# Causal masks of the second chunk moved from matmuls to GpSimd selects, and half-width scores for the last diagonal blocks

## The chip, the cores and the metric

One core of a Trainium2 chip runs the whole program. The metric is the device time of one execution in microseconds. The core has TensorE (PE in the rows, PEld for its weight loads), VectorE (DVE), ScalarE (ACT), GpSimd (POOL) and SyncE (SP), which here only issues transfers. Each engine works through its own instruction list strictly in the order in which it was written.

## The reference

The program is a layer on x of shape 4 x 1024 x 256. First comes a recurrence over the 1024 time steps, then attention with 16 heads of width 16, then four expert networks weighed by a gate:

```python
state = jnp.tanh(p_t + state)                      # 1024 steps, one after the other
scores = jnp.einsum('bhqd,bhkd->bhqk', q, k) * HD ** (-0.5)
scores = jnp.where(causal[None, None], scores, -jnp.inf)
attn = jax.nn.softmax(scores, axis=-1)
ao = jnp.einsum('bhqk,bhkd->bhqd', attn, v)...
x = x + ao
o0 = gelu(xf @ e0_up.T) @ e0_down.T;  o1 = silu(xf @ e1_w1.T) * (xf @ e1_w2.T) @ e1_down.T
o2 = gelu(gelu(gelu(xf @ e2_l1.T) @ e2_l2.T) @ e2_l3.T) @ e2_l4.T
o3 = gelu(gelu(xf @ e3_down.T) @ e3_up.T) @ e3_out.T
moe = wts[:, 0:1] * o0 + wts[:, 1:2] * o1 + wts[:, 2:3] * o2 + wts[:, 3:4] * o3
```

A query attends to the keys up to its own position only. That causal mask is what the change is about.

## The kernel before

Time is cut into four chunks of 256 steps, and with four batches that makes 16 units u of 256 rows. Chunk c holds the units 4c to 4c+3. Chunk 0 is laid out differently: its units hold 128 rows of two batches each. A unit goes through these items, named as in the code: `pgate` (VectorE multiplies the states by their gate, L1414, once the chunk's states are there), `ptr` (TensorE transposes the result, tensor G), the projections, keys and queries (`qk`, `kt`, `qt`), the row maxima of the scores (`mxm` on TensorE, `mxr` on VectorE, L1502), the scores again in transposed form (`sc`), their exponentials (`ex`, ScalarE L996), their product with the values (`av`), the gate, and the expert networks (`up`, `dn`, `gel` with Gelu, ScalarE L1021). The recurrence runs beside all that: `sadd` on GpSimd (L1703, 128x8) and `stanh` on ScalarE (L928) take turns 1023 times.

An item ("sc", u, g, kb) computes, for the four heads of group g of unit u, the scores of 128 keys (key block kb) against the unit's 256 queries: four matmuls of 64 rows and 256 columns (QT,KT in the rows), two for each half of the array's rows. Two of the key blocks of a unit of chunks 1 to 3 lie on the diagonal: r = kb - 2c = 0, where the first 128 queries are masked, and r = 1, where the first 128 queries see none of the keys and only the other 128 are masked and used. `ex` and `av` of r = 1 already work on the 128 later queries alone. The key blocks of an item lie in one of three buffers PT, which `sc` takes and `av` frees.

The mask is made in two ways. In chunks 0 and 1 TensorE adds a large negative triangle to the scores, with bf16 matmuls of 128 rows and 256 columns (maskk,identb; two for each diagonal block in chunk 1). In chunks 2 and 3 GpSimd sets the exponentials above the diagonal to zero with a select (item `msk`, L1710), between `ex` and `av`.

The order of each engine's list is made at build time by a planner, `arrange`: each item has a cost and a due time, and the planner plays the engines against each other and picks, whenever one is free, the ready item that is due first. Due times are START[u] plus an offset of the table AT for the kind of item and the chunk; STAY is a penalty for a change of the tile shape on TensorE (64 rows for scores, 128x32 for `av`, 128x128 for the rest) or of the activation table on ScalarE (exp and tanh against Gelu). What comes out is a fixed list for each engine with semaphore waits.

Of the kernel before, what the change touches and what calls it, by code (L numbers as in the profile page):

```python
# [14 lines left out]
L = 256  # L15
# [39 lines left out]
WINDOW, LOW, HIGH, FRESH = 3.413, 0.38, 0.75, 80.0  # L55

STALL = {"wsh": 0.3, "wsp": 0.45, "gll": 0.45, "kh": 0.12, "pgate": 0.15, "qq": 0.06, "hsc": 0.05, "fin": 0.05, "pln": 0.03, "pu": 0.03}
STAY = {"pe": 16.7, "act": 8.9}

START = (102.9, 140.3, 204.6, 251.3, 335.0, 429.5, 526.1, 598.9, 741.5, 802.0, 921.2, 978.2, 1089.0, 1179.7, 1287.1, 1381.6)  # L60
AT = {"piece": (39.4, 44.9, 92.6, 23.9),
      "post": (93.2, 49.6, -17.0, 3.1),
      "prep": (-51.0, -38.4, -68.0, -35.2),
      "value": (-95.0, 23.8, -123.9, -82.3),
      "key": (-43.2, -59.1, -16.5, -80.5),
      "query": (-41.3, -15.2, -108.7, -61.0),
      "max": (-17.8, -44.1, -58.3, -51.2),
      "maxima": (-1.8, 0.3, 14.4, 28.3),
      "bound": (89.2, -27.2, 53.0, 56.2),
      "score": (35.5, 43.9, 31.6, 47.9),  # L70
      "scores": (10.8, 11.3, 14.8, 8.7),
      "av": (16.9, -18.8, -3.1, 1.4),
      "merge": (20.7, -9.4, 0.4, 0.6),
      "out": (-126.5, -10.3, -47.2, -91.6),
      "gate": (-4.1, -106.5, -67.1, 55.1),
      "l1": (80.1, 225.4, 181.2, 220.9),
      "e0up": (150.5, 178.4, 131.2, 276.8),
      "l2": (216.7, 249.6, 193.5, 235.9),
      "e0dn": (276.2, 242.4, 399.5, 7.6),
      "e1": (250.8, 267.7, 297.6, 287.7),  # L80
      "l3": (312.5, 277.6, 195.7, 216.8),
      "e3dn": (206.3, 290.6, 219.8, 294.3),
      "e1dn": (324.7, 305.2, 239.5, 272.0),
      "l4": (309.9, 294.0, 253.9, 336.6),
      "e3up": (322.5, 265.2, 244.9, 238.0),
      "e3out": (277.8, 251.8, 317.6, 371.2),
      "fin": (272.9, 230.9, 245.5, 366.3)}


class Plan:  # L90
# [6 lines left out]
    def add(self, engine, key, us, due, *after, take=None, mode=None, lat=0.0):  # L97
        self.items[key] = (engine, us, due, dict(take or {}), mode, lat)
        self.left[key] = len(after)
        for a in after:  # L100
            self.feeds[a].append(key)
# [147 lines left out]
def arrange():  # L249
    P = Plan()  # L250
    add = P.add
# [26 lines left out]
    for n in range(2 * NCH):  # L278
        c, s = divmod(n, 2)
# [24 lines left out]
    for n in range(T):  # L304
        c, t = divmod(n, L)
# [12 lines left out]
    for u in range(NU):  # L318
        c, b = divmod(u, B)
        d0, at = START[u], {k: v[c] for k, v in AT.items()}  # L320
        d = d0 + at["post"]
        rows, nkb = tiles_of_time(u), key_blocks(u)
# [65 lines left out]
        for g in range(4):  # L388
            dg = d + at["scores"] * g
            add("sp", ("vl", u, g), 0.35, dg - 5, *[("vst", w) for w in keys_before(u)], *([("vl", *prior["vl"])] if "vl" in prior else []), lat=4.5, take={"VL": (("av", u, g, nkb - 1),)})  # L390
            prior["vl"] = (u, g)
            for h in range((nkb + 3) // 4):
                lastkb = min(4 * h + 3, nkb - 1)
                add("sp", ("kts", u, g, h), 0.35, dg - 5, *keys, *([("kts", *prior["kts"])] if "kts" in prior else []), lat=4.5, take={"KT": (("sc", u, g, lastkb),)})
                prior["kts"] = (u, g, h)
            for kb in range(nkb):
                r = kb - 2 * c if c else kb - u // 2 - 2
                mask = kb == u // 2 if c == 0 else r >= 0 and c < 2
                add("pe", ("sc", u, g, kb), (0.236 if c else 0.45) + (0.5 if mask else 0), dg, ("kts", u, g, kb // 4), ("mtd", u),
                    *([("sc", *prior["sc"])] if "sc" in prior else []),  # L400
                    mode="64", take={"P2": (("ex", u, g, kb),), "PT": (("av", u, g, kb),)}, lat=DRAIN)
                add("act", ("ex", u, g, kb), act(512 if r == 1 else 1024), dg, ("sc", u, g, kb), mode="exp")
                prior["sc"] = (u, g, kb)
                pt = ("ex", u, g, kb)
                if r >= 0 and c >= 2:
                    pt = ("msk", u, g, kb)
                    add("pool", pt, 0.75, dg, ("ex", u, g, kb))
                take = {"P1": (("avc", u, g),), "avbank": (("avc", u, g),), "AVS": (("mgt", u, g),)} if kb == 0 else None
                add("pe", ("av", u, g, kb), 0.222 if r == 1 else 0.434, dg + at["av"], pt, ("vl", u, g), *([("av", *prior["av"])] if "av" in prior else []),
                    mode="c32", take=take, lat=DRAIN)  # L410
                prior["av"] = (u, g, kb)
            add("dve", ("avc", u, g), dve(256), dg + at["merge"], ("av", u, g, nkb - 1))

            add("pe", ("mgt", u, g), 0.145, dg + at["merge"], ("avc", u, g), mode="128", lat=DRAIN,
                take={"P1": (("mgd", u, g),), **({} if g else {"AO": (("aot", u),)})})
            add("dve", ("mgd", u, g), 0.5, dg + at["merge"], ("mgt", u, g), *([("mgd", u, g - 1)] if g else []))
# [93 lines left out]
class Signals:  # L510
# [46 lines left out]
    def done(self, *key):  # L557
        name, value = self.value[key]
        return self.sem(name), value
# [25 lines left out]
def build(nc, A, out):  # L585
    ctx = ExitStack()
    with ctx:
        plan = arrange()
        S = Signals(nc, ctx, plan)
        done, of, freed, latest, place = S.done, S.of, S.freed, S.latest, plan.place  # L590
# [9 lines left out]
        def two(*key):  # L600
            i = place[key, "P2"]
            return PS[:, i:i + 2, :]
# [124 lines left out]
        def keys_of(buf, planes, n):  # L727
            return buf[:, 0:planes * n].rearrange("p (a k) -> p a k", a=planes)
# [309 lines left out]
        def _(eng):  # L1038
            pe = Engine(eng)

            def mm(o, l, r, start, stop, skip=False):
                return eng.matmul(o, l, r, start=start, stop=stop, skip_group_check=skip)  # L1042
# [4 lines left out]
            for key in plan.order["pe"]:  # L1047
                kind, a = key[0], key[1:]
# [6 lines left out]
                if kind == "htr":  # L1055
                    n, i = a
                    ps = two("htr", n, 0)
                    pe.wait_ge(*done("ident"))
                    pe.wait_ge(*done("hsc", n, i))
                    for kc in range(2):  # L1060
                        ins = tr(ps[:, kc, 128 * i:128 * i + 128], half(n)[:, i, 128 * kc:128 * kc + 128])
                    ins.then_inc(of(*key), 1)
                elif kind in ("hpx0", "hpx1"):
                    n, gate = a[0], int(kind[3])
                    ps = two(*key)
# [3 lines left out]
                    for m in range(2):  # L1069
                        col = 256 * gate + 128 * m  # L1070
                        for kc in range(2):
                            ins = mm(ps[:, m, :], wx[:, kc, col:col + 128], xn[:, kc, :], kc == 0, kc == 1)
                    ins.then_inc(of(*key), 1)
                elif kind == "ptr":
                    u = a[0]
                    gv, ps = G[place[("gl", u), "G"]], one(*key)
# [9 lines left out]
                    for s in range(2):  # L1086
                        for m in range(2):
                            ins = tr(ps[:, 256 * s + 128 * m:256 * s + 128 * m + 128], gv[:, m, 128 * s:128 * s + 128])
                    ins.then_inc(of(*key), 1)
                elif kind in ("qtr", "xtr"):  # L1090
                    u = a[0]
                    hv, ps = HA, one(*key)
# [5 lines left out]
                elif kind == "qk":  # L1098
                    u, s = a
                    ps = one(*key)  # L1100
# [8 lines left out]
                elif kind == "vm":  # L1109
                    u = a[0]  # L1110
# [47 lines left out]
                elif kind == "sc":  # L1158
# [1 line left out]
                    c = u // B  # L1160
                    n = min(512, 128 * key_blocks(u) - 512 * (kb // 4))
                    qt, kt = QT[place[("qt", u, 0), "QT"]], KT[place[("kts", u, g, kb // 4), "KT"]]
                    ps, r = two(*key), kb - 2 * c
                    pe.wait_ge(*done("mtd", u))
                    pe.wait_ge(*done("kts", u, g, kb // 4))
                    for par in range(2):
                        rows = slice(64 * par, 64 * par + 64)
                        for pl in range(2):
                            if c:
                                ins = mm(ps[:, par, 256 * pl:256 * pl + 256],  # L1170
                                         keys_of(kt, 2, n)[rows, pl, 128 * (kb % 4):128 * (kb % 4) + 128], qt[rows, 2 * g + pl, :],
                                         pl == 0, True, True)
                            else:
                                for i in range(2):
                                    ins = mm(ps[:, par, 256 * pl + 128 * i:256 * pl + 128 * i + 128],
                                             keys_of(kt[:, 512 * i:], 2, n)[rows, pl, 128 * kb:128 * kb + 128],
                                             qt[rows, 2 * g + pl, 128 * i:128 * i + 128], pl + i == 0, True, True)
                    masked = [u // 2 == kb, u // 2 == kb] if c == 0 else [c == 1 and r == 0, c == 1 and r == 1]
                    for i in range(2):
                        for par in range(2) if masked[i] else ():  # L1180
                            ins = mm(ps[:, par, :].rearrange("p (l q) -> p l q", l=2)[:, :, 128 * i:128 * i + 128], identb, maskk,
                                     False, True, True)
                    ins.then_inc(of(*key), 1)
                elif kind == "av":
# [3 lines left out]
                    q0 = 128 if c and r == 1 else 0  # L1188
                    ps, pt, vl = one("av", u, g, 0), PT[place[("sc", *a), "PT"]], VL[place[("vl", u, g), "VL"]]
                    pe.wait_ge(*done("vl", u, g))  # L1190
                    pe.wait_ge(*done("msk" if r >= 0 and c >= 2 else "ex", *a))
                    if c:
                        for j in range(4):
                            ins = mm(ps[32 * j:32 * j + 32, q0:L], vl[:, kb, NV * j:NV * j + 32], pt[:, j % 2, j // 2, q0:L],
# [545 lines left out]
```

## Time and profile before

| | us |
|---|---|
| median of 3 runs (1596.09 to 1600.81) | 1599.23 |
| the profiled execution | 1593.35 |
| its span, first to last instruction | 1591.6 |
| PE busy in the span | 1407.8 |
| DVE, ACT, POOL busy in the span | 1093.4, 970.3, 295.7 |

The mean granted TensorE clock of the profiled execution is 0.936 of full speed. Busy times are unions of overlapping instructions. Matmul durations include the pipeline's tail, so the price of a group of matmuls is read from the start of its first to the start of what follows it, not from its duration.

### The profile page before, as it was taken

How to read it: one execution, taken by the hardware profiler on the slowest of the kernel's cores; microseconds unless marked ns; L12 is line 12 of the kernel's file. 1: busy time of each engine (PE TensorE's matmuls, PEld its weight loads, DVE VectorE, ACT ScalarE, POOL GpSimd, SP SyncE). 2: the span in 40 equal slices, each digit the busy share in tenths (PEclk: the TensorE clock that was granted, in tenths of full speed). 3: DMA queues.
4: the chain of work that ended last, by engine and by line, in shares of the span. 5: the costliest groups of instructions: out<-in, count | busy, mean ns of one | idle time of the engine just before them, and what ended most of it. 6: DMA issues, size and time to landing. Idle time of an engine off the chain costs nothing. (4 is left out here: it accounts for less than half of the span.)

```text
span 1591.6 us, 33801 instructions
## 1 busy us (share of the span) xinstructions
PE 1407.8 (88%) x12384; PEld 1114.6 (70%) x12384; DVE 1093.4 (69%) x2916; ACT 970.3 (61%) x2106; POOL 295.7 (19%) x1114
## 2 busy tenths in 40 slices
PE   6905778999997899999998899999999999999987
PEld 3404567889885578778876577877777568876787
DVE  7776586654668876758888776858896778574242
ACT  2545465765556677876564756387456875658941
POOL 3343332123323222223330100000000000000000
PEclk9956578999997999999999999999999999999999
DMA  5585436754575546636657555565656657565443
GB/s 171 146 283 154 112 105 186 214 156 144 182 217 183 166 156 180 201 108 210 199 178 216 153 181 165 186 205 174 205 180 189 204 168 216 162 207 172 134 122 109
DMA packets 244276, 278.54 MB, mean 175 GB/s; under 512 B 37136, under 2 KB 167696, under 8 KB 243856
## 3 DMA queue, kind: packets, MB, share of 16 engines
q1 hardware_dynamic: 244112, 276.39, 56.3%
q8 instruction: 99, 1.62, 0.4%
q14 instruction: 65, 0.53, 0.1%
HBM read 234.18 MB, written 43.45 MB: 174 GB/s over the span
## 5 line engine op out<-in xcount | busy, mean ns | idle before, releaser
L928 ACT ACTIVATE PX<-AD 128x8 f32<-128x8 f32 x1023 | 219.2, 214 | 228.8 <-POOL AD L1703 226.7
L1703 POOL TENSOR_TENSOR AD<-PX 128x8 f32<-128x8 f32 x1023 | 246.3, 241 | 585.5 <-ACT PX L928 569.8
L996 ACT ACTIVATE work<-PS 128x1024 f32<-128x1024 f32 (+1 forms) x312 | 288.1, 958 | 89.5 <-PE PS L1042 88.1
L1502 DVE TENSOR_REDUCE mx<-PS 128x2 f32<-128x1024 f32 (+3 forms) x256 | 256.3, 1020 | 76.1 <-PE PS L1042 75.6
L1042 PE MATMUL PS<-work,vlx 128*32 128x256 f32 (+2 forms) x2816 | 236.3, 377 | 20.8 <-ACT work L996 9.0
L1042 PE MATMUL PS<-EP,u_e_l 128*128 128x256 f32 x1024 | 201.7, 291 | 10.5 <-DVE EP L1368 8.2
L1042 PE MATMUL PS<-WB,work 128*128 128x192 f32 x1024 | 187.3, 338 | 8.2 <-ACT work L1021 3.9
L1042 PE MATMUL PS<-EP,WB 128*128 128x256 f32 x640 | 182.6, 285 | 0.0
L1042 PEld LDWEIGHTS PS<-WB,work 128*128 128x128 f32 x1024 | 171.2, 196 | 15.7 <-issue 9.1
L1042 PE MATMUL PS<-KT,QT 64*128 64x512 f32 (+3 forms) x768 | 151.2, 432 | 30.9 <-DVE mx L1502 11.4
L1042 PEld LDWEIGHTS PS<-EP,u_e_l 128*128 128x128 f32 x1024 | 165.7, 194 | 18.2 <-issue 13.7
L1021 ACT ACTIVATE work<-PS 128x512 f32<-128x512 f32 x176 | 104.3, 596 | 113.6 <-PE PS L1042 112.1
L1042 PE MATMUL PS<-XF,WB 128*128 128x256 f32 x576 | 163.2, 283 | 0.0
L1042 PEld LDWEIGHTS PS<-work,vlx 128*32 128x32 f32 (+1 forms) x2816 | 87.6, 114 | 106.7 <-issue 55.8
L1710 POOL TENSOR_SCALAR_AFFINE_SELECT work<-work 128x512 f32<-128x512 f32 x64 | 43.3, 689 | 632.5 <-ACT work L996 632.4
L1042 PE MATMUL PS<-QT,KT 64*128 64x256 f32 (+1 forms) x1344 | 141.9, 314 | 14.9 <-ACT work L996 7.1
L1042 PEld LDWEIGHTS PS<-QT,KT 64*128 64x128 f32 x1344 | 97.9, 190 | 67.6 <-issue 44.5
L1042 PEld LDWEIGHTS PS<-KT,QT 64*128 64x128 f32 x768 | 72.9, 197 | 79.1 <-issue 29.6
L1042 PEld LDWEIGHTS PS<-EP,WB 128*128 128x128 f32 x640 | 124.8, 195 | 0.1
L1632 DVE SCALAR_TENSOR_TENSOR UU<-PS,wts,UU 128x192 f32<-128x192 f32 x128 | 47.3, 411 | 103.7 <-PE PS L1042 103.5
L1502 DVE TENSOR_REDUCE mxb<-PS 128x2 f32<-128x256 f32 (+3 forms) x128 | 104.7, 818 | 17.8 <-PE PS L1042 17.4
L1042 PEld LDWEIGHTS PS<-XF,WB 128*128 128x128 f32 x576 | 110.9, 193 | 0.0
(170 smaller groups left out, 2393.6 us busy)
## 6 DMA issues: line engine op xcount, KB each, us to landing
KT<-ktd SPq DMA_DIRECT2D x112, 512.0 KB, 4.7
WB<-wlo_e_l SPq DMA_DIRECT2D x160, 256.0 KB, 3.0
WB<-wlo_e_up SPq DMA_DIRECT2D x64, 256.0 KB, 3.0
ktd<-KTs SPq DMA_DIRECT2D x128, 128.0 KB, 2.3
WB<-wlo_e_w SPq DMA_DIRECT2D x64, 256.0 KB, 3.0
WB<-wdn_e_down SPq DMA_DIRECT2D x64, 192.0 KB, 2.8
KT<-ktd SPq DMA_DIRECT2D x48, 256.0 KB, 3.7
KT<-ktd SPq DMA_DIRECT2D x32, 384.0 KB, 3.8
```

What stands on the lines that cost most here:

```text
L928: eng.activation(cur, AD[n % 2], ACT.Tanh).then_inc(of(*key), 1)
L996: eng.activation(pt[:, :, :, q0:L], two("sc", *a).rearrange("p a (l q) -> p a l q", l=2)[:, :, :, q0:L], ACT.Exp).then_inc(of(*key), 1)
L1021: eng.activation(half_of(hidden(u, name), h), one("up", u, name, h), ACT.Gelu).then_inc(of(*key), 1)
L1042: return eng.matmul(o, l, r, start=start, stop=stop, skip_group_check=skip)
L1502: eng.tensor_reduce(o, two("mxm", *a)[:, :, 0:w], AX, ALU.max, negate=True).then_inc(of(*key), 1)
L1632: ins = eng.scalar_tensor_tensor(U, ps[:, t, 0:NO], wts[:, u % 4, t, e_:e_ + 1], U, ALU.mult, ALU.add)
L1703: eng.tensor_tensor(AD[n % 2], PX[c % 2][:, :, :, t], PX[(n - 1) // L % 2][:, :, :, (n - 1) % L], ALU.add).then_inc(of(*key), 1)
L1710: eng.affine_select(out=p, in_=p, compare_op=ALU.is_ge, fill=0.0, base=0, pattern=[[0, 2], [0, 2], [1, 128]], channel_multiplier=-1).then_ ...
```

## The change

The masks of chunk 1 are made like those of chunks 2 and 3: 32 `msk` items on GpSimd (4 units, 4 groups, 2 blocks) replace 64 mask matmuls, and `av` of these blocks waits for the select. The scores of all blocks with r = 1 in chunks 1 to 3 (48 items) are computed for the 128 later queries alone, so their four matmuls have 128 columns in place of 256. The planner is told so, and START, AT and STAY have new numbers throughout, which gives another order on every engine.

```diff
-STAY = {"pe": 16.7, "act": 8.9}
+STAY = {"pe": 18.5, "act": 7.0}
...
-START = (102.9, 140.3, 204.6, 251.3, 335.0, 429.5, 526.1, 598.9, 741.5, 802.0, 921.2, 978.2, 1089.0, 1179.7, 1287.1, 1381.6)
+START = (114.6, 163.8, 192.7, 269.5, 332.7, 421.8, 507.9, 597.9, 743.8, 801.4, 926.0, 996.4, 1096.7, 1187.3, 1295.6, 1383.6)
...
-                mask = kb == u // 2 if c == 0 else r >= 0 and c < 2
-                add("pe", ("sc", u, g, kb), (0.236 if c else 0.45) + (0.5 if mask else 0), dg, ("kts", u, g, kb // 4), ("mtd", u),
+                mask = c == 0 and kb == u // 2
+                add("pe", ("sc", u, g, kb), (0.45 if c == 0 else 0.18 if r == 1 else 0.236) + (0.5 if mask else 0), dg, ("kts", u, g, kb // 4), ("mtd", u),
...
-                if r >= 0 and c >= 2:
+                if r >= 0 and c:
                     pt = ("msk", u, g, kb)
                     add("pool", pt, 0.75, dg, ("ex", u, g, kb))
...
-                    ps, r = two(*key), kb - 2 * c
+                    ps, q0 = two(*key), 128 if c and kb == 2 * c + 1 else 0
...
-                                ins = mm(ps[:, par, 256 * pl:256 * pl + 256],
-                                         keys_of(kt, 2, n)[rows, pl, 128 * (kb % 4):128 * (kb % 4) + 128], qt[rows, 2 * g + pl, :],
-                                         pl == 0, True, True)
+                                ins = mm(ps[:, par, 256 * pl + q0:256 * pl + 256],
+                                         keys_of(kt, 2, n)[rows, pl, 128 * (kb % 4):128 * (kb % 4) + 128],
+                                         qt[rows, 2 * g + pl, q0:L], pl == 0, True, True)
...
-                    masked = [u // 2 == kb, u // 2 == kb] if c == 0 else [c == 1 and r == 0, c == 1 and r == 1]
-                    for i in range(2):
-                        for par in range(2) if masked[i] else ():
+                    for i in range(2) if c == 0 and u // 2 == kb else ():
+                        for par in range(2):
...
-                    pe.wait_ge(*done("msk" if r >= 0 and c >= 2 else "ex", *a))
+                    pe.wait_ge(*done("msk" if r >= 0 and c else "ex", *a))
```

TensorE's list before, at the diagonal blocks of the first group of unit 4 (`work,vlx` is `av`, `QT,KT` a score block, `maskk,identb` its mask):

```order
L1042 MATMUL PS<-EP,WB 128x256
L1042 MATMUL PS<-EP,u_e_up 128x256
L1042 MATMUL PS<-work,vlx 32x256 x4
L1042 MATMUL PS<-QT,KT 128x256 x4
L1042 MATMUL PS<-maskk,identb 128x2x128 x2
L1042 MATMUL PS<-work,vlx 32x256 x4
L1042 MATMUL PS<-QT,KT 128x256 x4
L1042 MATMUL PS<-maskk,identb 128x2x128 x2
L1042 MATMUL PS<-KT,QT 128x384 x2
L1042 MATMUL PS<-maskq,pick 128x64 x2
L1042 MATMUL PS<-maskn,pick 128x64 x2
```

The same place after (the second diagonal block is the one of 128x128, `QKP` are transposes of keys of another unit, `HA` those of a unit's rows):

```order
L1042 MATMUL PS<-work,vlx 32x256 x4
L1126 MATMUL PS<-identr,QKP 128x128 x8
L1042 MATMUL PS<-work,vlx 32x256 x4
L1042 MATMUL PS<-QT,KT 128x128 x4
L1042 MATMUL PS<-QT,KT 128x256 x4
L1042 MATMUL PS<-work,vlx 32x256 x4
L1045 MATMUL PS<-ident,HA 128x128 x4
L1042 MATMUL PS<-WB,work 128x192 x8
L1042 MATMUL PS<-work,vlx 32x128 x4
L1042 MATMUL PS<-QT,KT 128x256 x8
```

The masks are gone from the list, each `av` of a diagonal block stands farther behind its scores, and other work has come between them.

GpSimd's list before, from the recurrence's steps (TENSOR_TENSOR) to the end:

```order
L1703 TENSOR_TENSOR AD<-PX 128x8 x999
L1710 AFFINE_SELECT work<-work 128x4x128
L1703 TENSOR_TENSOR AD<-PX 128x8 x10
L1710 AFFINE_SELECT work<-work 128x4x128
L1703 TENSOR_TENSOR AD<-PX 128x8 x14
L1710 AFFINE_SELECT work<-work 128x4x128 x62
```

GpSimd's list after, from the same first steps, to the first selects of unit 5:

```order
L1702 TENSOR_TENSOR AD<-PX 128x8 x638
L1709 AFFINE_SELECT work<-work 128x4x128
L1702 TENSOR_TENSOR AD<-PX 128x8 x2
L1709 AFFINE_SELECT work<-work 128x4x128
L1702 TENSOR_TENSOR AD<-PX 128x8 x5
L1709 AFFINE_SELECT work<-work 128x4x128
L1702 TENSOR_TENSOR AD<-PX 128x8 x4
L1709 AFFINE_SELECT work<-work 128x4x128
L1702 TENSOR_TENSOR AD<-PX 128x8 x9
L1709 AFFINE_SELECT work<-work 128x4x128
L1702 TENSOR_TENSOR AD<-PX 128x8 x2
L1709 AFFINE_SELECT work<-work 128x4x128
```

Before, 62 of 64 selects stood behind the last step of the recurrence. After, 32 selects stand between step 638 and step 810, each in line with the steps.

TensorE's list before, where `ptr` of unit 8 stands (`ident,G`; it needs the states of steps up to 767):

```order
L1042 MATMUL PS<-maskn,pick 128x64 x2
L1042 MATMUL PS<-KT,QT 128x384 x2
L1042 MATMUL PS<-maskq,pick 128x64 x2
L1042 MATMUL PS<-maskn,pick 128x64 x2
L1045 MATMUL PS<-ident,G 128x128 x4
L1042 MATMUL PS<-work,vlx 32x256 x4
L1042 MATMUL PS<-KT,QT 128x512 x2
L1042 MATMUL PS<-maskq,pick 128x64 x2
L1042 MATMUL PS<-maskn,pick 128x64 x2
L1042 MATMUL PS<-QT,KT 128x256 x4
```

The same place after:

```order
L1042 MATMUL PS<-work,vlx 32x128 x4
L1042 MATMUL PS<-KT,QT 128x384 x2
L1042 MATMUL PS<-maskq,pick 128x64 x2
L1042 MATMUL PS<-maskn,pick 128x64 x2
L1045 MATMUL PS<-ident,G 128x128 x4
L1045 MATMUL PS<-ident,work 128x128 x2
L1042 MATMUL PS<-KT,QT 128x384 x2
L1042 MATMUL PS<-maskq,pick 128x64 x2
L1042 MATMUL PS<-maskn,pick 128x64 x2
```

The transpose has moved back. Before, 3 of unit 6's 8 diagonal score blocks stood ahead of it; after, 6 of them and their `av` do. ScalarE's list has 1 table load in front and then 129 switches between its two tables before, and 115 after; up to the first `ex` of unit 8 there are 39 loads before and 45 after.

## Rows read from the trace of the kernel before

**Rows 1.** Page, part 1: engine, busy us (share of the span), instructions.

```profile
PE 1407.8 (88%) x12384; PEld 1114.6 (70%) x12384; DVE 1093.4 (69%) x2916; ACT 970.3 (61%) x2106; POOL 295.7 (19%) x1114
```

**Rows 2.** By stretch: busy us (count) of PE, PEld, DVE, ACT, POOL; granted clock.

```profile
0.00:498.00 498.00, 386.58 (x2978) 316.47 (x2978) 331.64 (x1000) 271.63 (x907) 163.17 (x665) 0.84 0.58 173
498.00:707.00 209.00, 196.16 (x1881) 144.34 (x1881) 156.57 (x435) 156.01 (x376) 48.70 (x208) 0.98 0.53 164
707.00:842.00 135.00, 128.09 (x1046) 113.84 (x1045) 107.19 (x267) 82.82 (x253) 41.72 (x179) 0.96 0.62 192
1200.00:1500.00 300.00, 284.72 (x2798) 209.77 (x2798) 187.24 (x415) 213.39 (x250) 19.39 (x30) 0.99 0.57 184
```

**Rows 3.** Waits in 498:707: who waited for whom, us, times, longest.

```profile
ACT PX L928 <- POOL AD L1703: 30.0, 89, 1.1
```

**Rows 4.** TensorE's timeline at masked blocks: start us, us, instructions.

```profile
502.82 0.51 PE L1042 MATMUL PS<-QT,KT 64*128 64x256 f32 x4
...
503.58 0.64 PE L1042 MATMUL PS<-work,vlx 128*32 128x256 f32 x8
...
697.77 0.50 PE L1042 MATMUL PS<-QT,KT 64*128 64x256 f32 x4
698.21 0.39 PE L1042 MATMUL PS<-maskk,identb 128*128 128x256 bf16 x2
698.53 0.51 PE L1042 MATMUL PS<-QT,KT 64*128 64x256 f32 x4
698.97 0.39 PE L1042 MATMUL PS<-XF,u_e_w 128*128 128x256 f32 x1
...
706.41 0.51 PE L1042 MATMUL PS<-QT,KT 64*128 64x256 f32 x4
...
706.99 0.36 PE L1042 MATMUL PS<-EP,u_e_l 128*128 128x256 f32 x1
```

**Rows 5.** The same at blocks without a mask, 128 and 256 columns wide.

```profile
288.54 1.17 PE L1042 MATMUL PS<-QT,KT 64*128 64x128 f32 x16
289.64 0.61 PE L1042 MATMUL PS<-maskk,identb 128*128 128x256 bf16 x4
...
901.42 0.74 PE L1042 MATMUL PS<-QT,KT 64*128 64x256 f32 x8
902.09 0.39 PE L1042 MATMUL PS<-wqkv,hT 128*128 128x256 f32 x1
...
1056.99 0.51 PE L1042 MATMUL PS<-QT,KT 64*128 64x256 f32 x4
1057.42 0.64 PE L1042 MATMUL PS<-work,vlx 128*32 128x256 f32 x8
```

**Rows 6.** GpSimd's selects in chunks 2 and 3, and who waited for them.

```profile
L1710 POOL TENSOR_SCALAR_AFFINE_SELECT work<-work x64: 635/637/1192, 825.1 to 1515.0; 128x512 f32<-128x512 f32 x64
```

**Rows 7.** TensorE's waits over the whole span: us, times, longest us.

```profile
PE PS L1042 <- ACT work L996: 19.1, 34, 1.4
...
PE PS L1042 <- ACT work L1021: 5.9, 9, 1.5
...
PE PS L1042 <- POOL work L1710: 5.6, 10, 1.7
```

**Rows 8.** ScalarE's table loads in the groups by form.

```profile
L1021 ACT ACT_TABLE_LOAD x65 | 83.4, 1283 | 35.9 <-PE PS L1042 35.2
```

**Rows 9.** Recurrence to step 767, and what follows on VectorE and TensorE.

```profile
L928 ACT ACTIVATE PX<-AD x637: 198/216/228, 24.1 to 497.5; 128x8 f32<-128x8 f32 x160
...
L928 ACT ACTIVATE PX<-AD x767: 198/216/238, 24.1 to 621.4; 128x8 f32<-128x8 f32 x192
...
621.88 0.70 DVE L1414 SCALAR_TENSOR_TENSOR G<-G,PX 128x512 f32<-128x512 f32 x1
...
631.92 0.66 PE L1045 MATMUL PS<-ident,G 128*128 128x128 f32 x4
...
644.55 0.51 PE L1042 MATMUL PS<-QT,KT 64*128 64x256 f32 x4
```

More of the change, by code:

```diff
@@ L57 @@
 STALL = {"wsh": 0.3, "wsp": 0.45, "gll": 0.45, "kh": 0.12, "pgate": 0.15, "qq": 0.06, "hsc": 0.05, "fin": 0.05, "pln": 0.03, "pu": 0.03}
-STAY = {"pe": 16.7, "act": 8.9}
-START = (102.9, 140.3, 204.6, 251.3, 335.0, 429.5, 526.1, 598.9, 741.5, 802.0, 921.2, 978.2, 1089.0, 1179.7, 1287.1, 1381.6)
[L61 to L87, printed above, removed]
@@ new lines @@
+STAY = {"pe": 18.5, "act": 7.0}
+START = (114.6, 163.8, 192.7, 269.5, 332.7, 421.8, 507.9, 597.9, 743.8, 801.4, 926.0, 996.4, 1096.7, 1187.3, 1295.6, 1383.6)
+AT = {"piece": (-65.1, 79.3, 93.0, 117.5),
+      "post": (73.5, 53.5, -11.6, 4.0),
+      "prep": (-32.9, -50.6, -75.5, -31.9),
+      "value": (-168.0, 5.7, -122.1, -102.7),
+      "key": (-92.9, -70.4, 23.2, -60.9),
+      "query": (-70.1, -15.7, -105.7, -9.8),
+      "max": (-55.3, -48.9, -46.0, -51.3),
+      "maxima": (1.8, 4.8, 14.5, 33.1),
+      "bound": (97.6, -38.5, 63.2, 74.1),
+      "score": (20.8, 39.5, 20.4, 48.1),
+      "scores": (18.6, 9.7, 15.8, 8.7),
+      "av": (18.9, -22.6, 2.7, 0.5),
+      "merge": (36.4, -20.4, -11.9, 0.7),
+      "out": (-203.1, 8.4, -74.1, -92.8),
+      "gate": (-58.6, -112.8, -61.9, -36.5),
+      "l1": (38.7, 246.6, 204.8, 191.9),
+      "e0up": (141.5, 167.2, 99.3, 296.6),
+      "l2": (241.4, 262.9, 274.5, 274.1),
+      "e0dn": (304.8, 265.3, 456.7, -58.1),
+      "e1": (248.8, 254.1, 341.0, 226.9),
+      "l3": (253.5, 307.5, 179.0, 266.6),
+      "e3dn": (182.7, 315.9, 233.6, 257.0),
+      "e1dn": (285.7, 322.0, 304.5, 354.3),
+      "l4": (216.1, 314.5, 172.6, 308.5),
+      "e3up": (250.0, 261.2, 290.1, 275.3),
+      "e3out": (240.7, 251.3, 293.6, 381.5),
+      "fin": (203.7, 196.0, 239.1, 437.5)}
```

## The prediction, on record before the changed kernel was run

> **What bounds the kernel now.** I read the page's part 1 first. TensorE is busy for 1407.8 of 1591.6 us, and no other engine comes over 1094 [rows 1]. The table by stretch then says where this holds. Up to 498 us TensorE is busy for only 78% and its granted clock is 0.84. This is the part in which the recurrence hands out the first chunks, and the change hardly touches it. From 498 to 707 us, where all the diagonal blocks of chunk 1 are scored, TensorE is busy for 196.16 of 209 us at a clock of 0.98. From there on it stays at about 95% [rows 2]. So work taken from TensorE after 498 us is worth its time, as long as the work that is ready behind it fills the place. The second chain to watch is the recurrence, because GpSimd gets the new work. In the same stretch ScalarE waited 30.0 us for GpSimd's additions [rows 3]. The third thing is the place where the recurrence meets TensorE.
>
> **The masks that go.** A masked pair is priced from the start of its score block to the start of what follows. Before a 128x128 item this is 706.99 - 706.41 = 0.58 us, before an `av` 503.58 - 502.82 = 0.76, and before another score block 698.53 - 697.77 = 0.76 [rows 4]. An unmasked block takes 698.97 - 698.53 = 0.44 before a 128x128 item [rows 4] and 1057.42 - 1056.99 = 0.43 before an `av`, with a change of tile shape on either side. Two unmasked blocks in a row take 902.09 - 901.42 = 0.67 with the same two changes, so one block with one change is 0.34 [rows 5]. The mask costs little before 128x128 items, since it has that shape itself and the change is paid anyway. It costs more elsewhere, where the array goes to 128x128 and back. In the list of before 15 of the 32 masked blocks stand before a 128x128 item, 7 before an `av` and 10 before scores. The sum is 15 x 0.14 + 7 x 0.33 + 10 x 0.42 = 8.6 us. The bounds are 32 x 0.14 = 4.5 and 32 x 0.42 = 13.4 us.
>
> **The halved blocks.** The trace has no f32 score block of 128 columns in chunks 1 to 3, but unit 2 has such matmuls. Sixteen of them run from 288.54 to 289.64 us, and with about 0.1 us each for the way into and out of the tile shape they take 0.056 us apiece. Eight of 256 columns take 0.67 us from 901.42, less the same 0.2, so 0.059 apiece [rows 5]. Halving the columns therefore changes almost nothing, as something other than columns sets the pace. Four matmuls in 48 blocks give 192 x 0.003 = 0.6 us. The lower bound is nothing, the upper half of 0.236 us a block, 5.7 us. I take 0.6.
>
> The Trainium skill speaks against a gain here too: TensorE: Matmul & The Clock Gate, Back-to-back issue gap, says that in a stream of weight loads and matmuls both set the spacing, about 81 ns for each matmul at 128 columns. By that, a halved block would take 0.32 us, longer than the 0.24 that the trace shows for a full one, and the 48 blocks would cost about 4 us. The trace's 0.056 us apiece says otherwise, perhaps because two halves of the rows work side by side, so the sum goes by the row.
>
> **The selects.** One takes 0.637 us in the middle, 1.19 at most [rows 6], and 32 of them are 20.4 us of GpSimd, which is busy for 48.70 of 209 us there. That by itself is hidden. Each puts 0.64 us and a hop between `ex` and `av`. The 64 selects of before made TensorE wait 5.6 us in sum [rows 7], so 32 more cost 2.8 us. Lower bound nothing, upper 32 x 0.64 = 20.4 us, if nothing else could run on TensorE. I take 2.8, because the list of after has put other work between scores and `av`.
>
> The Trainium skill adds one doubt. GPSIMD Engine Reference, Specifications, says that GpSimd shares its SBUF interfaces with VectorE and contends with some of its instructions. The longest select of 1.19 us agrees with something of the kind. At that length throughout, the 2.8 us would be 5.2.
>
> **The new order.** The two lists can be counted. TensorE changes its tile shape 901 times before, masks included, and 885 after. The masks that go account for 10 x 2 + 7 = 27 of these, so the order itself adds 11, at 0.1 us each (0.44 less 0.34) +1.1 us. ScalarE has 130 table loads before and 116 after, at 1.283 us each [rows 8] 18 us less of ScalarE's time. ScalarE isn't the bound. TensorE waited 19.1 + 5.9 = 25.0 us for exponentials and Gelus [rows 7], with 130 loads among their causes, so 14 loads less are worth 14 x 0.19 = 2.7 us. The bounds are nothing and 18 us. What the order does otherwise to TensorE's 184 us without work can't be read from a list. I take it as zero and give it 10 us to either side in the range, some 5% of this idle time.
>
> **The sum.** -8.6 - 0.6 + 2.8 + 1.1 - 2.7 = -8.0 us. Against the profiled execution's 1593.35 us (span 1591.6) that is 1585.3. That execution ran below the lowest of the three timed runs, 1596.09, so I take the difference to their median: 1599.23 - 8.0 = 1591.2 us, half a per cent faster. What a measurement can tell from no change is about 0.3%, which is 4.8 us here.
>
> **Where a stall could come back.** VectorE's L1414 of unit 8 needs step 767. That step ran at 621.4, and L1414 started at 621.88, so it was waiting or all but; the transpose on TensorE followed at 631.92 [rows 9]. From step 637 at 497.5 the recurrence took 0.953 us a step. In the new list GpSimd has 22 selects between step 638 and step 767, and the transpose stands behind the sixth diagonal block of unit 6, whose scores ran at 644.55 [rows 9]. From 502.82 that is 141.7 us, less some 6 for the masks that are gone, so 136 us. The recurrence needs 129 x 0.953 = 123 us and 22 x 0.64 = 14, so 137 us. The order has moved by about as much as the selects cost, and the place is about as tight as before. If it is late, L1414 holds all of VectorE's list, the row maxima of unit 7 first, and with them TensorE.
>
> **Rivals.** (1) My forecast: masks off the bound engine, little given back, about 1591 us: 0.50. (2) The gain is given back: each select delays a step by 0.64 us and by one more turn between the engines, for which I take ScalarE's mean wait for an addition, 30.0 / 89 = 0.34 us [rows 3]; 22 x 0.98 = 22 us, the recurrence needs 145 us and is some 8 us late at L1414 of unit 8, and TensorE stands for it once. -8.0 + 8 = 0, so 1599 us, within 0.3% of before: 0.24. For it speaks that L1414 waited already; against it, that ScalarE waited for GpSimd for 30.0 us only and the steps have slack wherever ScalarE is at other work. (3) Slower: GpSimd's and ScalarE's lists lock at the 32 selects. A select stands ahead of a step, waits for an `ex` that comes later than planned, and ScalarE, whose next instruction is the step's tanh, waits too and so makes the following exponentials late. It decides from (8.0 + 2.8 + 4.8) / 32 = 0.49 us a select that reaches TensorE. With the full 0.98 it gives 32 x 0.98 - 10.8 = +20.6 us, 1620; with the 0.64 of the select alone +10, 1609. I give 0.21 to this and to a worse order together. Against it speaks that TensorE waited 5.6 us for 64 selects, 0.09 us each, though these stood on an engine without steps. (4) The halved blocks pay by columns and the loads saved on ScalarE count in full: -8.6 - 5.7 + 2.8 + 1.1 - 8 = -18, about 1581 us: 0.05, since rows 5 speak against the half of it.
>
> **How the numbers follow.** Faster by over 0.3% means below 1594.4: cases 1 and 4, 0.55. Within 0.3%: case 2, 0.24. Slower, above 1604.0: case 3, 0.21. The point is the likeliest case's 1591 us. The range goes from just below case 4, 1579, to 1607, short of case 3's two prices, which with what lies below 1579 leaves out no more than 2 in 10. The likeliest case's own range is 1583 to 1597.
>
> **What would show it.** In the changed kernel's profile the maskk matmuls are gone after 498 us. TensorE's busy time falls by some 8 to 10 us. Score blocks of 128 columns stand 0.2 us and more apart for four matmuls, not 0.12. GpSimd's selects are 96, those of chunk 1 each near 0.64 us, with TensorE's waits for them below 10 us. Step 767 lies near 635 to 640 us, L1414 of unit 8 right behind it, and TensorE's wait before that transpose is below 2 us. The prediction is wrong if that wait is several us, if ScalarE's wait for GpSimd in the stretch of chunk 1 has grown by more than 15 us and TensorE's for ScalarE with it, or if TensorE's idle time changed by over 10 us at places that have no diagonal block.

## The result, and the profile after

The changed kernel takes 1585.79 us (median of 6 runs, 1578.14 to 1589.69) against 1597.66 us for the kernel before beside it. The ratio is 0.9918, with a 95% interval of 0.9898 to 0.9938. The medians are 11.9 us apart and the ratio means 0.82% or 13 us less. That is inside the stated range, and faster as forecast, but more than the 8.0 us of the sum. The execution that was profiled, 1589.69 us, was the slowest of the six. The profiles of before and after therefore differ by less than the kernels do, 1591.6 against 1588.0 us of span. What follows from them is read stretch by stretch.

The page's part 1, and the waits of TensorE over the whole span (us, times, longest):

```profile
PE 1403.0 (88%) x12320; PEld 1108.8 (70%) x12320; DVE 1098.6 (69%) x2916; ACT 952.3 (60%) x2092; POOL 319.2 (20%) x1146
```

```profile
PE PS L1042 <- ACT work L996: 15.3, 32, 1.2
...
PE PS L1042 <- POOL work L1709: 4.9, 9, 0.8
...
PE PS L1042 <- ACT work L1021: 3.1, 8, 0.8
```

TensorE is busy for 4.8 us less than in [rows 1], where the prediction expected 8 to 10. It waits 4.9 us for all 96 selects, no more than for 64 before, and 15.3 + 3.1 = 18.4 us for ScalarE against 25.0 [rows 7].

Two of the stretches of [rows 2] (busy us of PE, PEld, DVE, ACT, POOL, then the granted clock):

```profile
498.00:707.00 209.00, 193.60 (x1802) 145.33 (x1801) 155.33 (x412) 151.97 (x340) 60.68 (x202) 0.93 0.52 160
707.00:842.00 135.00, 127.61 (x1003) 116.76 (x1003) 107.94 (x273) 77.22 (x252) 44.62 (x180) 0.97 0.64 197
```

In the stretch of chunk 1 TensorE is busy for 2.6 us less and its granted clock is 0.93, not 0.98. The place at which a stall could come back (the recurrence's step 767, L1413 of unit 8, the transpose), as in [rows 9]:

```profile
638.06 0.68 DVE L1413 SCALAR_TENSOR_TENSOR G<-G,PX 128x512 f32<-128x512 f32 x1
...
641.83 0.65 PE L1045 MATMUL PS<-ident,G 128*128 128x128 f32 x4
```

No idle time stands in brackets behind either row. Step 767 ended at 636.7 us, 1.3 us before L1413, VectorE was at a row maximum in between, and TensorE came to the transpose later still.

Now the end of the program. These are VectorE's rows before: the last item of unit 14 (L1632 to L1646), and then the piece EP of unit 15 (L1368), for which TensorE waits:

```profile
1534.89 0.74 DVE L1632 SCALAR_TENSOR_TENSOR UU<-PS,wts,UU 128x192 f32<-128x192 f32 x2 [1.44 <-PE PS L1042]
...
1540.35 0.69 DVE L1646 TENSOR_TENSOR UU<-UU,XR 128x512 f32<-128x512 f32 x1
...
1544.05 1.22 DVE L1368 TENSOR_TENSOR EP<-work,EP 128x1024 fp32r<-128x1024 f32 x1
```

The same work after:

```profile
1539.86 1.23 DVE L1367 TENSOR_TENSOR EP<-work,EP 128x1024 fp32r<-128x1024 f32 x1 [0.85 <-ACT EP L1028]
1541.00 0.74 DVE L1631 SCALAR_TENSOR_TENSOR UU<-PS,wts,UU 128x192 f32<-128x192 f32 x2
...
1545.22 0.69 DVE L1645 TENSOR_TENSOR UU<-UU,XR 128x512 f32<-128x512 f32 x1
```

Their order is reversed. TensorE's waits between 1500 and 1546 us before (us, times, longest), and the row of busy times behind the longest of them:

```profile
PE PS L1042 <- DVE EP L1368: 4.1, 1, 4.1
PE PS L1042 <- DVE work L1620: 0.7, 1, 0.7
PE PS L1042 <- ACT work L1021: 0.3, 1, 0.3
```

```profile
1545.40:1548.00 2.60, 2.59 (x12) 2.60 (x13) 0.00 (x0) 0.00 (x0) 0.00 (x0) 0.50 0.02 6
```

The granted clock was 1.00 from 1530 to 1540 us and 0.50 in these 2.6 us, the lower of TensorE's two levels (1.2 and 2.4 GHz). The first 13 matmuls behind the wait took 2.91 us, from 1545.41 to 1548.32. The same 13 took 1.53 us in the changed kernel, where no wait stands ahead of them. So the wait of 4.1 us cost 5.5. All four profiled kernels with the old order untouched have it, 4.07 to 4.09 us and then 2.91 us for the 13 matmuls.

After, all waits from 1500 us to the end:

```profile
PE PS L1042 <- DVE EP L1367: 2.2, 1, 2.2
PE PS L1042 <- ACT work L1021: 0.8, 1, 0.8
```

Both of these lie in the last 20 us, and the kernel before has them too (TensorE's timeline shows 2.22 and 0.78 us there). The 5.1 us between 1500 and 1546 are gone without a successor, and with them the 1.4 us of the slow clock.

### The profile page after: what moved, and what is told of

It is laid out like the page before. It is cut to its first block and busy times, and to the rows that moved or that the text cites. A ratio compares the mean times of both kernels' runs of the same rounds, so it can differ in the third digit from the quotient of the medians.

```text
span 1588.0 us, 33694 instructions
## 1 busy us (share of the span) xinstructions
PE 1403.0 (88%) x12320; PEld 1108.8 (70%) x12320; DVE 1098.6 (69%) x2916; ACT 952.3 (60%) x2092; POOL 319.2 (20%) x1146
## 5 line engine op out<-in xcount | busy, mean ns | idle before, releaser
L1702 POOL TENSOR_TENSOR AD<-PX 128x8 f32<-128x8 f32 x1023 | 250.4, 245 | 553.3 <-ACT PX L928 537.3
L1042 PE MATMUL PS<-work,vlx 128*32 128x256 f32 (+2 forms) x2816 | 240.6, 381 | 18.3 <-ACT work L996 7.5
L1042 PE MATMUL PS<-EP,u_e_l 128*128 128x256 f32 x1024 | 199.4, 289 | 6.9 <-DVE EP L1367 4.5
L1709 POOL TENSOR_SCALAR_AFFINE_SELECT work<-work 128x512 f32<-128x512 f32 x96 | 63.8, 674 | 638.1 <-ACT work L996 637.9
L1042 PE MATMUL PS<-WB,work 128*128 128x192 f32 x1024 | 181.2, 330 | 3.6 <-ACT work L1021 1.3
L1042 PE MATMUL PS<-EP,WB 128*128 128x256 f32 x640 | 182.3, 285 | 0.0
L1042 PE MATMUL PS<-KT,QT 64*128 64x512 f32 (+3 forms) x768 | 151.9, 434 | 27.8 <-DVE mx L1501 12.9
L1042 PEld LDWEIGHTS PS<-EP,u_e_l 128*128 128x128 f32 x1024 | 164.0, 192 | 14.8 <-issue 10.3
L1042 PEld LDWEIGHTS PS<-WB,work 128*128 128x128 f32 x1024 | 164.9, 190 | 10.0 <-issue 4.0
L1042 PE MATMUL PS<-XF,WB 128*128 128x256 f32 x576 | 163.5, 284 | 0.0
L1042 PEld LDWEIGHTS PS<-work,vlx 128*32 128x32 f32 (+1 forms) x2816 | 87.6, 115 | 103.3 <-issue 49.6
L1042 PE MATMUL PS<-QT,KT 64*128 64x256 f32 (+1 forms) x1344 | 142.7, 315 | 15.9 <-ACT work L996 7.1
L1042 PEld LDWEIGHTS PS<-QT,KT 64*128 64x128 f32 x1344 | 99.9, 193 | 66.3 <-issue 45.6
L1042 PEld LDWEIGHTS PS<-KT,QT 64*128 64x128 f32 x768 | 72.8, 197 | 75.6 <-issue 27.1
L1042 PEld LDWEIGHTS PS<-EP,WB 128*128 128x128 f32 x640 | 124.3, 194 | 0.0
L1042 PEld LDWEIGHTS PS<-XF,WB 128*128 128x128 f32 x576 | 111.2, 193 | 0.1
```

The costliest lines, as they stand in the source:

```text
L1702: eng.tensor_tensor(AD[n % 2], PX[c % 2][:, :, :, t], PX[(n - 1) // L % 2][:, :, :, (n - 1) % L], ALU.add).then_inc(of(*key), 1)
L1709: eng.affine_select(out=p, in_=p, compare_op=ALU.is_ge, fill=0.0, base=0, pattern=[[0, 2], [0, 2], [1, 128]], channel_multiplier=-1).then_ ...
```

## Experiments

The edit (new masks, half-width blocks) and the new order come together. The first four kernels take them apart. Theory A: the gain is the work taken from TensorE. Theory B: the new order gives half of it or more. All ratios are to the kernel before, run on the same chip in the same rounds.

**The old order with the new masks and half-width blocks.** The list of each engine is that of before, and each select goes behind the addition that stands ahead of its exponential. The rest of the edit is that of the change:

```diff
...
+        for k in pool:
+            new.append(k)
+            if k[0] == "sadd" and k[1] in ex:   # ex: step -> selects whose exponential follows it on ScalarE
+                new += ex.pop(k[1])
+        plan.order["pool"] = new
...
```

> The order of before on every engine, with the new masks (32 selects set into GpSimd's list right behind the recurrence step that stands ahead of their exponential) and the halved blocks. Theory A (the gain is the work taken from TensorE, the new order gives nothing): -8.6 us for the masks, -3.1 us for the halved blocks (0.065 us each in the changed kernel's trace), +2.8 us of waits for selects, so about 9 us under before, 1589. Theory B (the new order gives half of the 12 us): the waits for selects eat more, as av stands close behind its scores in the old order; 0 to 5 us under before, 1593 to 1598.

Measured: 1596.23 us, ratio 0.9984 (0.9964 to 1.0004). The edit alone gives 2.6 us, and its interval goes from nothing to 5.8 us. TensorE's waits in 498:707 of its profile (L1055 is L1042 of the kernel before, L1722 the select):

```profile
PE PS L1055 <- POOL work L1722: 6.2, 9, 1.4
PE PS L1055 <- ACT work L1009: 6.1, 8, 1.6
```

In the kernel before TensorE waits there for no select, and for ScalarE's exponentials

```profile
PE PS L1042 <- ACT work L996: 7.1, 11, 1.4
```

so some 5 us of waits have come in for the masks that went.

**The new order with the old masks and full-width blocks.**

```diff
+        plan.order["pool"] = [k for k in plan.order["pool"] if k[0] != "msk" or k[1] >= 2 * B]
...
-                    ps, q0 = two(*key), 128 if c and kb == 2 * c + 1 else 0
+                    ps, q0 = two(*key), 0
...
-                    for i in range(2) if c == 0 and u // 2 == kb else ():
-                        for par in range(2):
+                    r = kb - 2 * c
+                    masked = [u // 2 == kb, u // 2 == kb] if c == 0 else [c == 1 and r == 0, c == 1 and r == 1]
+                    for i in range(2):
+                        for par in range(2) if masked[i] else ():
...
-                    pe.wait_ge(*done("msk" if r >= 0 and c else "ex", *a))
+                    pe.wait_ge(*done("msk" if r >= 0 and c >= 2 else "ex", *a))
```

> The order of the changed kernel on every engine, with the mask matmuls of chunk 1 and the full-width blocks of before. Theory A: as before, 1597. Theory B: the order alone is worth some 6 us, so 1591 or less.

Measured: 1586.39 us, ratio 0.9921 (0.9899 to 0.9942). The order gives 12.6 of 1598 us (9 to 16 by the interval), with the masks of chunk 1 still made by matmuls and no half-width block anywhere. Theory A falls. Theory B holds, and the order is worth about twice the 6 us that it named.

**The changed kernel with full-width blocks** (`q0` set to 0 as above).

> The changed kernel with full-width blocks at r = 1; only the halving is undone. By the changed kernel's trace 48 x 0.065 = 3.1 us slower than it, 1589; by the prediction's 0.6 us no difference, 1586.

Measured: 1583.79 us, ratio 0.9918 (0.9892 to 0.9943), as the changed kernel. The rows do show shorter blocks. One with a change of shape on either side takes 1099.45 - 1099.08 = 0.37 us, against 0.43 in [rows 5]:

```profile
1099.08 0.44 PE L1042 MATMUL PS<-QT,KT 64*128 64x128 f32 x4
1099.45 0.64 PE L1042 MATMUL PS<-work,vlx 128*32 128x256 f32 x8
```

Matched block by block between this run's trace and the changed kernel's, 40 of the 48 half-width blocks are shorter from start to start, 37 of them by 0.06 to 0.07 us. The other 8 are not, as something else held the next item there. A block with no change of shape on either side takes 0.175 us at 128 columns and 0.24 at 256. The blocks together are 2 to 3 us shorter. The timing is too coarse to see it, so whether it reaches the end stays open.

**The changed kernel with mask matmuls in chunk 1, half-width blocks kept.** The diff is that of the new order with the old masks, without the lines of `q0`.

> The changed kernel with the masks of chunk 1 by matmuls again (half-width blocks kept, no selects in chunk 1, the order kept). Theory A: the masks' 8.6 us less 2.8 us of waits come back, so 6 us slower than the changed kernel, 1592. Theory B, or selects that cost nothing: 4 us or 9 us and more.

Measured: 1587.8 us, ratio 0.9935 (0.9911 to 0.9960), 2 to 3 us above the changed kernel. The two intervals together allow from nothing to 8 us, so theory A's 6 us are not excluded by this run alone. By the medians and ratios the edit gives no more than some 3 us in either order. In the new order the whole edit is the difference between 0.9921 and 0.9918, with some 5 us to either side.

Next, what takes the masks' gain. Theory S: the selects give it back. Theory R: something else than TensorE sets the pace in the stretch of chunk 1.

**The changed kernel without its selects of chunk 1.**

```diff
-                    pe.wait_ge(*done("msk" if r >= 0 and c else "ex", *a))
+                    pe.wait_ge(*done("msk" if r >= 0 and c >= 2 else "ex", *a))
+        plan.order["pool"] = [k for k in plan.order["pool"] if k[0] != "msk" or k[1] >= 2 * B]
```

> The changed kernel without its 32 selects of chunk 1, which so goes unmasked; av waits for the exponentials alone. Theory S (selects eat what the masks' removal gives): some 5 us under the changed kernel, 1580. Theory R (in that stretch something else than TensorE ends last, so neither masks nor selects count much): as the changed kernel, 1585 to 1586.

Measured: 1588.37 us, ratio 0.9928 (0.9897 to 0.9958), not faster than the changed kernel. In the new order the selects cost nothing that can be measured; by the intervals it is 4 us at most.

**The changed kernel with each of these selects twice.**

```diff
+                    if u < 2 * B:
+                        step(eng.affine_select(out=p, in_=p, ...))
+                        pool.wait_ge(clink, steps[0])
                     eng.affine_select(out=p, in_=p, ...)
```

> The changed kernel with each select of chunk 1 made twice, one after the other. That adds 32 x 0.64 = 20.5 us to GpSimd, where the recurrence's additions stand in the same list. Theory S: 5 us and more slower than the changed kernel, 1590 and up; if the recurrence sets the end of that stretch, up to 20 us. Theory R with slack on GpSimd: within 2 us of it.

Measured: 1596.92 us, ratio 0.9979 (0.9960 to 0.9999), some 10 us slower than the changed kernel. The first 20.5 us on GpSimd cost nothing measurable, and the second about half of themselves (5 to 14 us by the intervals). TensorE's wait for selects in 498:707 of its profile, 1.2 us in the changed kernel:

```profile
PE PS L1042 <- POOL work L1713: 6.3, 8, 2.2
```

The two kernels have the same list on TensorE, so the loss can be followed along it. At the changed kernel's 450 us this run is 1.9 us behind at the same instruction, at 550 us 7.0, at 633 us 8.4, and from 754 to 1560 us between 8.3 and 9.3. Most of the loss falls in the stretch with the selects. ScalarE waits 36.5 us for GpSimd's additions there, against 24.7 in the changed kernel.

**The old order with each mask matmul of chunk 1 twice.**

```diff
+                            for _ in range(2 if c == 1 else 1):
                                 ins = mm(ps[:, par, :]..., identb, maskk, False, True, True)
```

> The kernel before with each mask matmul of chunk 1 made twice (a second large negative number changes nothing after the exponential). That adds 64 matmuls of 256 columns without a change of tile shape, 64 x 0.11 to 0.12 = 7 to 8 us of TensorE's time between 498 and 707 us. If TensorE's time is the bound there it is 7 to 8 us slower than before, 1605; if something else sets the pace there it is 0 to 3 us slower, 1598 to 1601.

Measured: 1604.8 us, ratio 1.0034 (1.0015 to 1.0054), 5.4 us slower (2.4 to 8.6) for 7 to 8 us of matmuls.

**The old order without the mask matmuls of chunk 1, and nothing in their place.**

```diff
-                    masked = [u // 2 == kb, u // 2 == kb] if c == 0 else [c == 1 and r == 0, c == 1 and r == 1]
+                    masked = [u // 2 == kb, u // 2 == kb] if c == 0 else [False, False]
```

> The kernel before without the mask matmuls of chunk 1 and with nothing in their place (that chunk goes unmasked), order kept. The prediction's 8.6 us for the masks: 1591 if before is 1600. If TensorE's time there is worth the same share as in the run with the masks twice (about 0.7), 6 us. If it is worth little when taken away, 0 to 3 us, as in the run with selects in the old order.

Measured: 1595.61 us, ratio 0.9964 (0.9944 to 0.9985), 5.8 us faster (2.4 to 9.0). From the start of the score block to the start of what follows, the 32 blocks took 7.0 us less in this run's trace than in that of before. So TensorE's time in that stretch counts, added or taken away, and theory R falls. The two runs point at some three quarters of it, but neither interval excludes all of it. In the old order the selects and the half-width blocks together would then cost some 3 us (0.9984 against 0.9964), where `av` stands close behind its scores. The intervals overlap, so this is not shown by the times; the 5 us of waits above agree with it.

Last, the order. Theory B1: the gain lies in the last 55 us. Theory B2: it is spread over the whole program. TensorE's lists can be matched item by item between kernels of either order. The time from the same amount of work done to the same amount done later then scatters by several us between executions up to about 1400 us, but hardly after it. To compare the ends, TensorE's list is counted back from its last matmul. Each matmul is priced by the lower quartile of the distances from its start to the next, taken after 1200 us from all traces. The stretch between 60 and 23 us of remaining work then took 47.9, 49.0, 48.0 and 48.1 us in the four profiled kernels with the old order untouched, and 37.9 to 38.3 us in seven with the new end. With mean distances as prices the difference is about 7 us and not 10. The waits and the slow clock that are gone there account for 5.1 + 1.4 = 6.5 us of it. Over the earlier stretches the differences between the two orders go both ways, and no part of the gain could be placed there.

**The kernel before with one more dependency.** The e3_out product of unit 14 follows the e2_l1 products of unit 15. The planner then puts VectorE's last item of unit 14 behind EP of unit 15 by itself:

```diff
+            add("pe", ("dn", u, name), ..., *([("up", 15, "e2_l1", 1)] if (u, name) == (14, "e3_out") else []), mode="128", ...
```

> The kernel before with one more dependency for the planner: the e3_out product of unit 14 comes after the e2_l1 products of unit 15, as in the new order. Everything up to the last 55 us stays. Theory B1 (the gain is in the last 55 us: there the profiles differ by 7 us, and TensorE's 4.08 us wait for VectorE's EP is gone in the new order): 4 to 7 us under before, 1591 to 1594. Theory B2 (the gain is spread over the whole order and the tail is chance): no difference, 1598.

Measured: 1594.92 us, ratio 0.9976 (0.9955 to 0.9996), 3.8 us. The interval is 0.6 to 7.2 us. The stretch above takes 44.0 us. The waits of 4.1 and 0.3 us are gone, but between 1500 and 1546 us a new one has come in beside the 0.7 us of before:

```profile
PE PS L1042 <- DVE XF L1359: 2.0, 1, 2.0
```

The sum of what the trace shows is 4.1 + 1.4 + 0.3 - 2.0 = 3.8 us, as measured. The new order does not have the wait of 2.0 us: there the gate's product (gwp,XF) and unit 15's first pieces have other work of unit 14 ahead of them.

**The changed kernel with this one thing reversed.**

```diff
+        up("e2_l1", ("xfl", u), "gel", ..., *([("dn", 14, "e3_out")] if u == 15 else []), take=...
```

> The changed kernel with the e3_out product of unit 14 ahead of the e2_l1 products of unit 15 again, and so VectorE's last item of unit 14 ahead of the EP piece of unit 15. Theory B1: 4 us or more slower than the changed kernel, ratio to before 0.994 to 0.996. Theory B2: 0.992, no difference.

Measured: 1592.16 us, ratio 0.9949 (0.9932 to 0.9967), 5 us of the gain gone (1 to 9 by the intervals of the two). The stretch takes 43.3 us in place of some 38. TensorE's waits between 1500 and 1555 us:

```profile
PE PS L1042 <- ACT work L1021: 2.9, 1, 2.9
PE PS L1042 <- DVE EP L1367: 0.7, 1, 0.7
```

This is not the old wait put back. Most of it stands ahead of the e3_out product itself, which waits for its own Gelu on ScalarE. The row of that product in this run, and then in the changed kernel:

```profile
1538.91 4.52 PE L1042 MATMUL PS<-WB,work 128*128 128x192 f32 x16 [2.86 <-ACT work L1021]
...
1537.84 2.84 PE L1042 MATMUL PS<-WB,work 128*128 128x192 f32 x16
```

Behind the wait the product takes 1.7 us longer, at a granted clock of 0.59 from 1538.9 to 1543.1 us. The waits and the slow clock come to 2.9 + 0.7 + 1.7 = 5.3 us. What the product's new place gives, work for TensorE during a wait or a shorter list on VectorE ahead of EP, was not timed apart: both move together in these two runs.

**The changed kernel with one more of the kind.** The e2_l4 product of unit 15 follows e3_down, so that its 2.5 us cover the wait of 2.2 us that was left:

```diff
+            add("pe", ("dn", u, name), ..., *([("up", 15, "e3_down", 0)] if (u, name) == (15, "e2_l4") else []), mode="128", ...
```

> The changed kernel with one more dependency: the e2_l4 product of unit 15 comes after its e3_down product, so that TensorE has 2.5 us of work during the 2.2 us in which it waited for EP 15 us before the end. If waits in the tail count in full, 2.2 us less than the changed kernel, ratio 0.990 to 0.991; no difference otherwise.

Measured: 1584.33 us, ratio 0.9901 (0.9872 to 0.9929), the fastest of all. Against the changed kernel's 0.9918 the step is as expected in size, but not beyond the intervals. The trace shows that the wait of 2.2 us is gone. Of the two waits in the last 20 us only the one of 0.8 us for ScalarE stays.

**The changed kernel with the old START, AT and STAY.** The planner knows the new costs and places the selects, by the old due times.

```diff
-STAY = {"pe": 18.5, "act": 7.0}
+STAY = {"pe": 16.7, "act": 8.9}
-START = (114.6, 163.8, ...)
+START = (102.9, 140.3, ...)
```

> The changed kernel with START, AT and STAY of before: the planner knows the new costs and the selects, but its due times are the old ones. If the new masks and half-width blocks are what makes it faster, as the changed kernel, 0.992. If the new tables are, 0.996 to 1.000, the last 55 us near the old ones.

Measured: 1666.35 us, ratio 1.0421 (1.0393 to 1.0450), some 67 us slower than before. That was outside everything expected. The mean granted clock of its profile is 0.912 against 0.936 before. The row of busy times from 1500 us to the end shows where a part of the loss lies:

```profile
1500.00:1664.00 164.00, 136.91 (x1206) 112.03 (x1202) 53.58 (x183) 93.09 (x115) 7.43 (x12) 0.94 0.40 123
```

TensorE stands idle for 27 us of the last 164, and the ends of the units have drifted. Here the due times fitted to the old costs did not fit the new ones, though the costs differ by a few tenths of a us an item. Which decisions of the planner tipped was not followed up, so why it is so much stays open.

## Why the prediction was right and wrong

**The step that failed** is the one on the new order: "What the order does otherwise to TensorE's 184 us without work can't be read from a list. I take it as zero". It is the main term. The order alone gives 12.6 us (0.9921, 9 to 16 us by the interval), of which 7 to 10 lie in the last stretch but one, between 60 and 23 us of remaining work. There 5.1 us of waits are gone and 1.4 us of slow clock behind the longest. A single product's place accounts for 4 to 5 us (0.9976, and 0.9949 against 0.9918). Where the rest of the 12.6 us lies is open, and part of it may be chance: the executions of the new order with the old masks had a mean clock of 0.9363 against 0.9335 beside them, which at 0.95 us for 0.001 (last section) is worth some 2.7 us, an estimate. The trace and the lists held the main part. The trace of before shows a wait of 4.1 us for EP, 46 us before the end, with VectorE busy on unit 14's last item shortly ahead of EP. The list of after shows that item behind EP, and the e3_out product where the wait was. That a wait in the last units counts at least in full, as nothing else is ready there, fits the runs above. I looked for a place where a stall could come back, and not for one where a stall goes.

**The masks** were priced at 8.6 us. Alone they are worth 5.8 (0.9964, 2.4 to 9.0 us). The trace of that run gives 7.0 us from start to start, so the price was near. Block by block the prices were less even: six of the 15 ahead of a 128x128 item gave 0.20 to 0.23 and not 0.14, those ahead of the row maxima's scores gave less than 0.42 as often as not, and some gave nothing, as the next item waited anyway.

**The selects** were taken at 2.8 us. In the new order they cost nothing measurable (0.9928 without them), though 2.8 us are not excluded, and in the old one a few us. The reason for the lower end was named, other work between scores and `av`. The doubt on the shared interfaces (the Trainium skill, GPSIMD Engine Reference, Specifications) did not matter in size: the 96 selects took 0.674 us on the mean and 1.12 at most, against 0.689 and 1.19 for the 64 before.

**The halved blocks** were taken at 0.6 us. The rows show 0.06 us a block, 2 to 3 us in all, about half-way to the upper bound. The reading that halving "changes almost nothing" was wrong: four matmuls without a change of shape take 0.175 us at 128 columns and 0.24 at 256, so 0.044 and 0.06 apiece. The price of 0.056 at 128 columns came from unit 2, whose sixteen matmuls stand in chunk 0 under other conditions. The rule of the Trainium skill (TensorE: Matmul & The Clock Gate, Back-to-back issue gap), by which such a block would have become longer, is not what these rows show. Timed, the halving gives 0.9918 against 0.9918.

**The table loads** fell from 130 to 116 as counted, and TensorE's waits for ScalarE from 25.0 to 18.4 us. Whether any of this reached the end is not shown, as no gain could be placed ahead of the last 60 us of TensorE's work.

**The rivals.** The forecast had step 767 at 635 to 640 us, and it came at 636.7. The second rival had L1413 of unit 8 some 8 us late, and it was not late. (Behind step 638 and ahead of addition 767 there are 21 selects, not 22, which changes 0.6 us.) With the selects twice the step came at 645.1 us and the kernel lost 10 us, but not at that place either. L1413 again had no idle time before it, and TensorE came to the transpose at 650.15 us with no wait for it, 8.3 us later than in the changed kernel. The loss was there already. It is the third rival's path, in small: TensorE's waits for selects grew by 5 us and ScalarE's for additions by 12. The third, engines locked at the selects, would have decided from 0.49 us a select that reaches TensorE. In the changed kernel ScalarE's wait for GpSimd in the stretch was 24.7 us against 30.0 and did not grow. That the direction came out right is in part luck: the edit gave less than its terms, 0 to 3 us, and the term taken as zero gave the rest.

## What to carry to other kernels

When a change comes with a new order, time the new order with the old work and the old order with the new work before believing in either. Read the last units' waits first, one by one. Here one of 4.1 us cost more than itself, as TensorE ran at half its clock behind it, and an item of an earlier unit on VectorE stood ahead of the last chain. A product of that unit moved into the wait took most of it away. Due times fitted to one set of costs may not suit another, even a close one.

## What the runs showed of the hardware

The spread of one kernel's executions goes with TensorE's granted clock. Over 136 timed executions of ten kernels (the kernel before, the changed one, those of the experiments up to the mask matmuls twice, and the kernel before with one more dependency), the deviations of time and mean clock from their kernel's mean have a correlation of -0.75, with 0.95 us for each 0.001 of mean clock. The changed kernel's fastest, 1578.14 us, had 0.939, its slowest, 1589.69 us, 0.933. So the clock goes with about half of the variance within a kernel. It is not the difference between before and after: 75 executions of the kernel before had a mean of 0.9334, the six of the changed kernel 0.9342, which is worth under 1 us. In the stretch of chunk 1 the changed kernel's profile had 0.93 against 0.98, but the new order with mask matmuls and half-width blocks had 0.93 there too, and that with the old masks and full width 0.96, while other profiles with the old order had 0.94 to 0.96.

A wait is not always followed by a slow clock. The wait of 2.2 us in the last 20 us stands in 13 of the 14 profiles. Behind it the 13 next matmuls took 1.55 to 1.61 us in seven of them and 1.98 to 2.91 us in six. Behind the wait of 4.1 us they took 2.91 us in the four kernels with the old order, and 2.41 us in the one with the old tables.

A change of tile shape had a steady price in the changed kernel's rows. Four score matmuls of 128 columns took 0.175 us from start to start with no change on either side, 0.275 with one ahead of them, and 0.37 with one ahead and one behind. At 256 columns it was 0.24, 0.34 and 0.435.
